# A graph network's node passes become one dense chain, and its edge targets travel as one row per edge

## The chip, the core and the metric

The kernel runs on one core of a Trainium2 chip. The metric is the device time of one execution in microseconds. TensorE (PE) multiplies matrices, VectorE (DVE) and ScalarE (ACT) work elementwise, GpSimd (POOL) issues the indirect DMAs here, and SyncE (SP) issues the plain ones.

## The reference

50,000 nodes with 128 features, 25,000 edges sorted by destination `dst`. Four layers follow one another, each as `x = x + layer(relu(layernorm(x)))`:

```python
h = relu(layernorm(x)); x = x + L0(h)      # GINE
msg = relu(h[src] + edge_attr); agg = segment_sum(msg, dst)
y = relu((h + agg) @ W1.T + b1) @ W2.T + b2;  L0 = batchnorm over nodes(y)

h = relu(layernorm(x)); x = x + L1(h)      # two GATv2 convolutions, 4 heads
for layer in (1, 2):                       # with self loops; h is updated by each
    xl, xr = h @ Wl, h @ Wr                # 128 -> 4 x 128
    e = sum(leaky_relu(xl[src] + xr[dst]) * att); alpha = segment_softmax(e, dst)
    out = segment_sum(alpha * xl[src], dst).mean(heads) + bias
    h = h + layernorm(out) * g + be        # the kernel adds this and applies relu after layer 1

h = relu(layernorm(x)); x = x + L2(h)      # GAT, 4 heads of 64, then an MLP 256 -> 256 -> 128
h = relu(layernorm(x)); x = x + 0.5 * segment_mean(h[src], dst)
```

About 25,000 destinations were drawn from 50,000 nodes, so most nodes have no incoming edge. For such a node every segment sum is zero: its own softmax weight in a convolution is 1, and the attention layer gives it a constant vector.

## The kernel before

Everything is float32. Nodes are padded to 50,176 and handled in 98 tiles of 512 rows (128 partitions x 4), edges to 25,088 in 49 tiles of 512. The program is a sequence of phases, with a barrier after each (`Phase`), so that two phases don't overlap: `prepare_indices`, `gine_edges`, `gine_mlp`, `gine_finish`; for each convolution `conv_logits`, `edge_softmax`, `conv_aggregate`, `conv_nodes`; then `gat_logits`, `edge_softmax`, `gat_aggregate`, `gat_nodes`, and `mean_edges`. Within a phase each engine runs its own stream in order, and semaphores tie them together; `pipeline` writes the steps of several tiles interleaved, each with a lag.

The logits phases gather the rows of both ends of each edge from the table H in DRAM (`gather`, L186, four indirect DMAs of 128 rows for each end), turn them with TensorE transposes, multiply (`z_self`, `z_edge`), and reduce with the attention vectors (`dots`, L862, 32 weight columns for each head, side by side). The aggregate phases weigh the projected rows, turn them, sum each segment with a running scan on DVE (L1213, L1720), turn the sums back and scatter the last row of each segment to the table AGG (`scatter_last`, L192). The node phases (`conv_nodes`, `gat_nodes`) then stream all 98 node tiles: load H and AGG (and X), project and add, normalize, store H (and X). So each layer passes over all nodes once. `mean_edges` adds its rows to `out` with an accumulating indirect DMA (L1880). The attention's MLP runs over the edge tiles inside `gat_aggregate` (L1641, L1651).

A float32 matmul shows in the trace as two instructions, a transpose as one.

## Time and profile before

| | us |
|---|---|
| median of two runs | 6023.07 (6015.77 to 6030.36) |
| span of the profiled execution | 6037.5 |
| PE busy | 3381.0 (56%) |
| DVE busy | 3709.0 (61%) |
| ACT busy | 2564.7 (42%) |
| GpSimd busy | 3636.7 (60%) |

The phases begin at (us from the start of the span): `gine_edges` 28, `gine_mlp` 612, `gine_finish` 943, `conv_logits` 1242.5, `edge_softmax` 1765, `conv_aggregate` 1816, `conv_nodes` 2156; layer 1 of the convolution: 2617, 3138, 3190, 3526; `gat_logits` 4069, `edge_softmax` 4577, `gat_aggregate` 4624, `gat_nodes` 5098, `mean_edges` 5409 to 6037.5. No engine is busy for more than 61% of the whole; the limit is another one in each phase, so the shares of the whole say little and the stages have to be read one by one.

### The profile page before, as it was taken

To read this page: it belongs to the slowest core of one execution; us is meant where nothing else is said; L and a number is where in the kernel's file an instruction comes from. 1 tells how busy PE (TensorE), PEld (TensorE's weight loads), DVE (VectorE), ACT (ScalarE), POOL (GpSimd) and SP (SyncE) were. 2 spreads that over 40 slices of the span, in tenths; PEclk is the share of its full clock that TensorE was granted. 3 is DMA by queue.
4 is the path that set the end of the run, shared out by engine and by line. 5 is a ranking of instruction groups with operands and counts; after the bars stand their busy time and mean duration, and the time that the engine had idled before them with its cause. 6 is when DMAs were issued, how large, how long until landed. Compare 5 with 4: busy or idle time off the path is not lost. (4 is left out here: it accounts for less than half of the span.)

```text
span 6037.5 us, 71358 instructions
## 1 busy us (share of the span) xinstructions
PE 3381.0 (56%) x13980; PEld 1953.5 (32%) x13980; DVE 3709.0 (61%) x10702; ACT 2564.7 (42%) x5746; POOL 3636.7 (60%) x3368
## 2 busy tenths in 40 slices
PE   1221674369968944469978944434445996003332
PEld 0111232223325534423334534421113774002221
DVE  2332898956668979966658969981114555982221
ACT  1222897856641246656651247771111222650100
POOL 4777343467745666667744666657772444448887
PEclk9999996589989977779988966656667998555555
DMA  7332777932214245522212257752221112983343
GB/s 244 93 93 74 234 254 284 368 99 55 55 40 158 80 148 172 173 70 55 55 45 67 79 185 245 248 197 54 54 54 46 53 54 93 341 299 63 61 64 50
DMA packets 531584, 778.51 MB, mean 129 GB/s; under 512 B 162156, under 2 KB 217736, under 8 KB 528752
## 3 DMA queue, kind: packets, MB, share of 16 engines
q1 hardware_dynamic: 427952, 620.88, 30.7%
q0 software_dynamic: 103488, 156.17, 10.8%
q14 instruction: 111, 0.91, 0.0%
q8 instruction: 33, 0.54, 0.0%
HBM read 475.60 MB, written 312.09 MB: 130 GB/s over the span
## 5 line engine op out<-in xcount | busy, mean ns | idle before, releaser
L919 DVE TENSOR_TENSOR conv_logits_leaky<-conv_logits_z,conv_logits_sloped 128x512 f32<-128x512 f32 x784 | 542.4, 692 | 242.9 <-ACT conv_logits_sloped L882 237.6
L1314 PE MATMUL conv_nodes_o_ps<-wmean,conv_nodes_hT 128*128 128x128 f32 x1568 | 318.9, 366 | 454.4 <-ACT conv_nodes_hT L1378 427.0
L882 ACT ACTIVATE conv_logits_sloped<-conv_logits_z 128x512 f32<-128x512 f32 x784 | 468.3, 597 | 220.9 <-PE conv_logits_z L845 119.9
L192 POOL DMA_INDIRECT AGG<-conv_aggregate_rows,conv_aggregate_idx x392 | 385.1, 982 | 261.7 <-ACT conv_aggregate_rows L1177 166.3
L186 POOL DMA_INDIRECT conv_logits_hd<-H,conv_logits_idx x392 | 372.2, 949 | 127.7 <-issue 117.9
L186 POOL DMA_INDIRECT conv_logits_hs<-H,conv_logits_idx x392 | 372.1, 949 | 119.5 <-issue 119.2
L1314 PEld LDWEIGHTS conv_nodes_o_ps<-wmean,conv_nodes_hT 128*128 128x128 f32 x1568 | 271.0, 261 | 519.9 <-ACT conv_nodes_hT L1378 458.9
L1908 PE MATMUL mean_edges_turned<-mean_edges_ident,mean_edges_hs 128*128 128x128 f32 x196 | 54.6, 434 | 685.6 <-DMA mean_edges_hs<-H,mean_edges_idx 685.6
L1286 POOL TENSOR_TENSOR conv_nodes_agg<-conv_nodes_agg,conv_nodes_bias 128x512 f32<-128x512 f32 x196 | 248.5, 1268 | 310.8 <-DVE conv_nodes_scaled L1347 146.2
L1141 PE MATMUL conv_aggregate_y<-wl,conv_aggregate_diff 128*128 128x512 f32 x784 | 393.5, 627 | 31.8 <-DVE conv_aggregate_part L1204 31.8
L246 ACT ACTIVATE conv_nodes_scaled<-conv_nodes_o,conv_nodes_norm_shift,conv_nodes_norm_rstd 128x128 f32<-128x128 f32 x784 | 322.8, 482 | 170.5 <-DVE conv_nodes_norm_shift L241 165.1
L1204 DVE SCALAR_TENSOR_TENSOR conv_aggregate_part<-conv_aggregate_y,conv_aggregate_alpha,conv_aggregate_part 128x128 f32<-128x128 f32 x1176 | 358.5, 347 | 20.6
L845 PE MATMUL conv_logits_z<-conv_logits_hdT,wsum 128*128 128x512 f32 x784 | 366.0, 610 | 1.4 <-ACT conv_logits_hdT L876 1.4
L192 POOL DMA_INDIRECT AGG<-gat_aggregate_rows,gat_aggregate_idx x196 | 192.5, 982 | 268.4 <-ACT gat_aggregate_rows L1673 221.8
L853 PE MATMUL conv_logits_z<-diffT,wl 128*128 (+1 forms) x784 | 352.9, 593 | 0.0
L1880 POOL DMA_INDIRECT out<-mean_edges_rows,mean_edges_idx x196 | 308.1, 1572 | 59.7 <-issue 57.9
L1942 DVE TENSOR_TENSOR_SCAN mean_edges_sumT<-mean_edges_keep,mean_edges_sumT,mean_edges_turned 128x512 f32<-128x512 f32 x49 | 62.7, 1280 | 435.7 <-PE mean_edges_turned L1908 435.7
L1964 ACT ACTIVATE mean_edges_rows<-mean_edges_back,mean_edges_half 128x128 f32<-128x128 f32 x196 | 55.9, 368 | 527.0 <-PE mean_edges_back L1920 286.6
L192 POOL DMA_INDIRECT AGG<-gine_edges_rows,gine_edges_idx x196 | 207.0, 1056 | 102.3 <-issue 100.1
L1908 PEld LDWEIGHTS mean_edges_turned<-mean_edges_ident,mean_edges_hs 128*128 128x128 f32 x196 | 35.0, 217 | 705.1 <-issue 487.7
L1167 ACT ACTIVATE conv_aggregate_alpha<-conv_aggregate_alpha_ps 128x16 f32<-128x16 f32 x98 | 17.9, 183 | 520.8 <-DVE conv_aggregate_part L1204 456.1
L186 POOL DMA_INDIRECT gine_edges_hs<-x,gine_edges_idx x196 | 202.3, 1032 | 61.2 <-issue 58.8
(241 smaller groups left out, 10015.2 us busy)
## 6 DMA issues: line engine op xcount, KB each, us to landing
conv_nodes_h<-H SPq DMA_DIRECT2D x196, 256.0 KB, 2.7
conv_nodes_agg<-AGG SPq DMA_DIRECT2D x196, 256.0 KB, 3.0
AGG<-gine_edges_zero SPq DMA_DIRECT2D x14, 1792.0 KB
gine_mlp_x<-x SPq DMA_DIRECT2D x98, 256.0 KB, 2.7
gine_mlp_agg<-AGG SPq DMA_DIRECT2D x98, 256.0 KB, 3.2
YT<-gine_mlp_yT SPq DMA_DIRECT2D x98, 256.0 KB, 3.2
gine_finish_x<-x SPq DMA_DIRECT2D x98, 256.0 KB, 3.9
gine_finish_yT<-YT SPq DMA_DIRECT2D x98, 256.0 KB, 5.0
```

The source lines that it names most:

```text
L186: return pool.indirect_dma_start(out=out, out_offset=None, in_=table, in_offset=bass.IndirectOffsetOnAxis(ap=index, axis=0))
L192: return pool.indirect_dma_start(out=table, out_offset=bass.IndirectOffsetOnAxis(ap=index, axis=0), in_=rows, in_offset=None, bounds_check ...
L246: last = act.activation(out[:, a, :], x[:, a, :], func, bias=self.shift[k][:, a:a + 1], scale=self.rstd[k][:, a:a + 1])
L845: pe.matmul(z[h][:, :], g.wsum[:, h * D:(h + 1) * D], hdT[slot(k)][:, :], start=True, stop=True).then_inc(z_done[0], 1)
L853: pe.matmul(z[h][:, :], g.wl[:, h * D:(h + 1) * D], g.diffT[:, bass.ds(n * TILE, TILE)], start=False, stop=True, skip_group_check=True).th ...
L882: act.activation(sloped[H * j + h][:, :], z[h][:, :], ACT.Copy, scale=SLOPE).then_inc(sloped_made[j], 1)
L919: dve.tensor_tensor(leaky[H * j + h][:, :], z[h][:, :], sloped[H * j + h][:, :], ALU.max).then_inc(leaky_made[j], 1)
L1141: pe.matmul(y[s][:, :], diff[slot(k)][:, s * P:(s + 1) * P], g.wl[:, :], start=True, stop=True).then_inc(y_done, 1)
L1204: last = dve.scalar_tensor_tensor(out=out, in0=yh, scalar=a, in1=out, op0=ALU.mult, op1=ALU.add)
L1286: pool.tensor_tensor(flat(agg[r]), flat(agg[r]), bias[:, :], ALU.add).then_inc(agg_made, 1)
L1314: last = pe.matmul(o_ps[k % 2][:, a, :], hT[k % 2][:, a * P:(a + 1) * P], g.wmean[:, :], start=True, stop=True)
L1880: pool.indirect_dma_start(out=g.out[:, :], out_offset=bass.IndirectOffsetOnAxis(ap=idx[k][:, 12 + s:13 + s], axis=0), in_=rows[k][:, s, :] ...
```

## The change

Nodes are split in two kinds. A new phase `spread` takes every node through the two convolutions, the attention and the last norm as if it had no incoming edge, in one pass over the 98 node tiles with no return to DRAM between the layers. Nodes with incoming edges are wrong in it and are overwritten: their state is carried as one row per edge (each edge holds a copy of its destination's state), in transposed tiles in DRAM (HDT, X1DT, X2DT), and two new phases, `conv_update` after each `conv_aggregate` and `gat_update` after `gat_aggregate`, update these rows over the 49 edge tiles. `conv_nodes` and `gat_nodes` are gone. `spread` also gathers and turns the destination rows once, and stores for each edge tile the matrix `same` (edge i and j have the same destination) for each block of 128 edges. The aggregates multiply by `same` instead of scanning and scattering; what crosses a block's edge is added in the update phases by small matmuls (`ends`, `ind`). Norms are taken with a centering matrix and a matmul by a column of 1/128, instead of DVE's statistics. A table POS, filled in `gine_finish` by 196 indirect DMAs of 64-byte rows, tells where the current row of a node is; `spread` looks it up for each edge's source (196 more). The logits phases then gather only sources. `conv_logits` splits leaky_relu into a linear part (`lin`, one more matmul) and a relu. `mean_edges` adds the base row on DVE and overwrites rows of `out` with a plain scatter. The loops of the new phases are written out in full, with no loop on the chip. `make_weights` prepares all weights once. `gine_edges` and `gine_mlp` are as before.

```diff
 def gine_finish(nc, g):
...
-                def add_beta(k, i):
-                    pool.tensor_tensor(x1_beta[r][:, :, :], x1[r][:, :, :], beta[:, :, :], ALU.add).then_inc(shifted_made, 1)
+                    if k == 0 and isinstance(i, int) and i == 0:
+                        sp.wait_ge(self_made, 1)
+                        sp.dma_start(g.POS.rearrange("(p j) w -> p j w", p=P), self_row[:, :, :]).then_inc(self_out, 16)
...
+                make_identity(pool, ident, ident_made, cleared)
+                pool.iota(self_row[:, :, :], pattern=[[1, rows_each], [0, 16]], base=0, channel_multiplier=rows_each).then_inc(self_made, 1)
+                pool.iota(edge_row[:, :, :, :], pattern=[[TILE, g.NTE], [1, SUB], [0, 16]], base=g.NP, channel_multiplier=SUB).then_inc(edge_made, 1)
+                pool.wait_ge(self_out, 16)
+                wait_alone(pool, edge_made, 1, own)
+                for n in range(g.NTE):
+                    for s in range(SUB):
+                        scatter_last(pool, g.POS[:, :], g.idx[:, n, 8 + s:9 + s], edge_row[:, n, s, :], g.NP - 1).then_inc(g.placed, 16)
...
+def spread(nc, g):
+                for u in range(E2):
+                    n, col = u // 2, 4
+                    if u >= 7:
+                        wait_alone(pool, e_done, u - 6, own)
+                    for s in range(SUB):
+                        gather(pool, fetched[u % 7][:, s, :], (g.X if u % 2 else g.H)[:, :], g.idx[:, n, col + s:col + s + 1]).then_inc(fetched_in[u % 7], 16)
+                    for s in (0, 1) if u % 2 == 0 else (2, 3):
+                        gather(pool, pos[:, n, s, :], g.POS[:, :], g.idx[:, n, s:s + 1]).then_inc(g.looked, 16)
+                wait_alone(pool, g.looked, 16 * SUB * g.NTE, own)
+                pool.tensor_copy(g.idx[:, :, 12:16], pos[:, :, :, 0]).then_inc(pos_copied, 1)
+                pool.wait_ge(pos_copied, 1)
...
+                def variances(t):
+                    if t == 2:
+                        pe.wait_ge(V_set, 1)
+                    past(pe, sqrt_made, t - 2)
+                    for lag, sq, made, c in ((2, sq0, sq0_made, 0), (5, sq1, sq1_made, 4), (7, sq3, sq3_made, 8), (7, sq2, sq2_made, 12)):
+                        j = t - lag
+                        if 0 <= j < N:
+                            pe.wait_ge(made, j + 1)
+                            for a in range(SUB):
+                                last = pe.matmul(V[:, c + a:c + a + 1], sq[j % 2][:, a * P:(a + 1) * P], g.mean_col[:, :], start=True, stop=True)
+                    last.then_inc(V_done, 1)
...
+                def centered(out, rows):
+                    for a in range(SUB):
+                        last = pe.matmul(out[:, a * P:(a + 1) * P], rows[:, a * P:(a + 1) * P], g.center[:, :], start=True, stop=True)
+                    return last
+                def g3(j):
+                    t = j + 7
+                    past(pe, t0_made, upto(t - 1))
+                    pe.wait_ge(x3_made, j + 1)
+                    alone(t, h4_made, j)
+                    centered(Ga, x3T[j % 3]).then_inc(g3_done, 1)
...
+                def oX(j):
+                    t = j + 6
+                    pe.wait_ge(x3_made, j + 1)
+                    past(pe, sq0_made, upto(t))
+                    alone(t, sq2_made, j)
+                    pe.matmul(Oa[:, :], g.center[:, :], x3T[j % 3][:, :], start=True, stop=True).then_inc(oX_done, 1)
+                def e_turn(u):
+                    if u >= E2:
+                        return
+                    pe.wait_ge(fetched_in[u % 7], fetched0 + 64 * (u // 7 + 1))
+                    past(pe, a0_made, u - 2)
+                    alone(u, a1_made, u - 5)
+                    alone(u, eT_made, u)
+                    turn(T0, flat(fetched[u % 7])).then_inc(e_done, 1)
+                steps = [(6, t1T), (6, x1T), (0, h1T_), (2, g0), (5, g1), (1, out0), (3, t0T), (4, out1), (4, rA_), (7, g3), (7, g2),
+                         (7, r3), (6, oX), (0, e_turn)]
...
+                def squares(j):
+                    act.wait_ge(oX_done, j + 1)
+                    act.activation(sq3[j % 2][:, :], Oa[:, :], ACT.Square).then_inc(sq3_made, 1)
+                    act.activation(sq2[j % 2][:, :], Oa[:, :], ACT.Square, bias=g.ncc[:, :]).then_inc(sq2_made, 1)
+                def copy_e(u):
+                    if u >= E2:
+                        return
+                    act.wait_ge(e_done, u + 1)
+                    past(act, eT_out[u % 3], 16 * (u // 3))
+                    act.activation(eT[u % 3][:, :], T0[:, :], ACT.Copy).then_inc(eT_made, 1)
+                steps = [(0, copy_h1T), (1, square0), (3, relu_a0), (4, square1), (4, copy_rA), (6, squares), (0, copy_e)]
...
 def conv_logits(nc, g, layer):
...
-                        gather(pool, hd[k][:, s, :], g.H[:, :], idx[k][:, 4 + s:5 + s]).then_inc(rows_in[k], 16)
-                        gather(pool, hs[k][:, s, :], g.H[:, :], idx[k][:, s:s + 1]).then_inc(rows_in[k], 16)
+                    for s in range(SUB):
+                        gather(pool, hs[n % 7][:, s, :], table[:, :], g.idx[:, n, col + s:col + s + 1]).then_inc(rows_in[n % 7], 16)
...
+                def dot_edge(n):
+                    past(pe, logit_made[1], n)
+                    pe.matmul(dots[1][:, :], g.lin[layer][:, :, :], g.arena[:, n * TILE:(n + 1) * TILE], start=True, stop=True)
+                    pe.wait_ge(edge_made, n + 1)
+                    pe.wait_ge(edges_made, (H - 1) * (n + 1))
+                    for h in range(H):
+                        last = pe.matmul(dots[1][32 * h:32 * h + 32, :], g.att[layer][:, h, :], above[H + h][:, :],
+                                         start=False, stop=True, tile_position=(0, 32 * h), skip_group_check=True)
+                    last.then_inc(dots_done[1], 1)
+                sweep(N, [(1, z_self), (2, dot_edge), (0, turn), (1, z_edge), (1, dot_self)])
...
 def conv_aggregate(nc, g, layer):
...
+                def project(n):
+                    for s in range(SUB):
+                        past(pe, yw_made, SUB * (n - 1) + s + 1)
+                        pe.matmul(y[s][:, :], g.arena[:, n * TILE + s * P:n * TILE + (s + 1) * P], g.wlc[layer][:, :],
+                                  start=True, stop=True).then_inc(y_done, 1)
+                def collect(n):
+                    pe.wait_ge(same_in[n % 4], 16 * (n // 4 + 1))
+                    past(pe, agg_made, n - 1)
+                    for s in range(SUB):
+                        pe.wait_ge(yw_made, SUB * n + s + 1)
+                        for h in range(H):
+                            last = pe.matmul(agg[n % 2][:, s * P:(s + 1) * P], yw[(SUB * n + s) % 8][:, h * D:(h + 1) * D],
+                                             same[n % 4][:, s * P:(s + 1) * P], start=(h == 0), stop=(h == H - 1))
+                    last.then_inc(agg_done, 1)
+                sweep(N, [(0, turn_alpha), (0, project), (1, collect)])
...
+def conv_update(nc, g, layer):
...
+                def project(n):
+                    pe.wait_ge(hdT_in[n % 6], 16 * (n // 6 + 1))
+                    pe.wait_ge(ind_in[n % 4], 16 * (n // 4 + 1))
+                    past(pe, o_made, n)
+                    pe.matmul(O[:, :], g.wmc[layer][:, :], hdT[n % 6][:, :], start=True, stop=False)
+                    pe.wait_ge(endsT_made, n + 1)
+                    pe.matmul(O[:, :], endsT[n % 2][:, :], ind[n % 4][:, :], start=False, stop=True).then_inc(O_done, 1)
...
+                for at in range(N + 2 + tail + 2):
+                    if 0 <= at - 3 < N:
+                        turn_t(at - 3)
+                    if 2 <= at < N + 2 + tail:
+                        variance(at)
+                    if 0 <= at - 2 < N:
+                        turn_o(at - 2)
+                    if at < N:
+                        turn_ends(at)
+                    if 0 <= at - 1 < N:
+                        project(at - 1)
+                    if final:
+                        if 0 <= at - 5 < N:
+                            center_rows(at - 5)
+                        if 0 <= at - 4 < N:
+                            center_x(at - 4)
+                        if 0 <= at - 6 < N:
+                            turn_rows(at - 6)
+                    elif 0 <= at - 4 < N:
+                        turn_h(at - 4)
...
+def gat_update(nc, g):
...
+                def center_x(n):
+                    pe.wait_ge(x3_made, min(n + 2, N))
+                    pe.matmul(O[:, :], g.center[:, :], x3T[n % 3][:, :], start=True, stop=True).then_inc(X_done, 1)
...
+                sweep(N, [(5, variance), (1, carry(0)), (5, center_rows), (5, turn_x), (1, carry(1)), (2, first), (3, second), (4, center_x), (0, turn_ends)])
...
 def mean_edges(nc, g):
...
-                            pool.indirect_dma_start(out=g.out[:, :], out_offset=bass.IndirectOffsetOnAxis(ap=idx[k][:, 12 + s:13 + s], axis=0),
-                                                    in_=rows[k][:, s, :], in_offset=None, compute_op=ALU.add).then_inc(added[k], 16)
+                        scatter_last(pool, g.out[:, :], g.idx[:, n, 8 + s:9 + s], rows[n % 7][:, s, :], g.NP - 1).then_inc(placed[n % 7], 16)
...
+        steps = [prepare, make_weights, gine_edges, gine_mlp, gine_finish, spread,
+                 lambda nc, g: convolution(nc, g, 0), lambda nc, g: convolution(nc, g, 1), attention, mean_edges]
```

Two places in the program, all on TensorE. First the end of a convolution. Before, the seam between the last edge tile of `conv_aggregate` and `conv_nodes` (`partT` and `back` turn the segment sums there and back, `turned` is a PSUM bank with the turned node tile, `o_ps` the projection):

```order
L1156 MATMUL conv_aggregate_back<-conv_aggregate_ident,conv_aggregate_sumT 128x128 x4
L1148 MATMUL conv_aggregate_partT<-conv_aggregate_ident,conv_aggregate_part 128x128 x4
L1156 MATMUL conv_aggregate_back<-conv_aggregate_ident,conv_aggregate_sumT 128x128 x8
L1082 UNCONDITIONAL_BRANCH
L1297 UNCONDITIONAL_BRANCH
L1306 MATMUL conv_nodes_turned<-conv_nodes_ident,conv_nodes_h 128x128 x8
L1314 MATMUL conv_nodes_o_ps<-wmean,conv_nodes_hT 128x128 x4
L1306 MATMUL conv_nodes_turned<-conv_nodes_ident,conv_nodes_h 128x128 x4
```

Now, at the place of `conv_nodes`, `conv_update` over the 49 edge tiles, here for layer 0 and one tile (R, T and Q are turned rows, F the turned ends, O the projection with what is carried over, V the variance):

```order
L1637 MATMUL conv_update_R<-kept_ident,conv_update_o 128x128 x4
L1644 MATMUL conv_update_F<-kept_ident,conv_update_ends 8x128
L1650 MATMUL conv_update_O<-conv_update_hdT,kept_wmc 128x512
L1652 MATMUL conv_update_O<-conv_update_ind,conv_update_endsT 128x512
L1637 MATMUL conv_update_Q<-kept_ident,conv_update_hT 128x128 x4
L1637 MATMUL conv_update_T<-kept_ident,conv_update_t 128x128 x4
L1663 MATMUL conv_update_V<-kept_mean_col,conv_update_sq 128x1 x4
```

and the node tiles in `spread` (V, Ga, Gb, Oa and Ob are PSUM banks; T stands for T0, T1 and T2 by turns), one tile's turn from the variances on; three groups of four transposes into T stand ahead of it:

```order
L994 MATMUL spread_V<-kept_mean_col,spread_sq 128x1 x16
L956 MATMUL spread_Ga<-kept_ident,spread_o 128x128 x4
L956 MATMUL spread_Gb<-kept_ident,spread_o 128x128 x4
L1014 MATMUL spread_Oa<-spread_h1T,kept_wmc 128x512
L956 MATMUL spread_T<-kept_ident,spread_t 128x128 x4
L1027 MATMUL spread_Ob<-spread_hAT,kept_wmc 128x512
L956 MATMUL spread_T<-kept_ident,spread_hAT 128x128 x4
L1037 MATMUL spread_Ga<-kept_center,spread_x3T 128x128 x4
L1037 MATMUL spread_Gb<-kept_center,spread_x2T 128x128 x4
L956 MATMUL spread_T<-kept_ident,spread_x3T 128x128 x4
L1064 MATMUL spread_Oa<-spread_x3T,kept_center 128x512
L956 MATMUL spread_T<-kept_ident,spread_fetched 128x128 x4
```

Where a node tile had two groups for each convolution, one turn of `spread` now has fifteen, among them sixteen matmuls with one moving column; and the edge tiles got seven groups of their own.

Second, TensorE's stream in the attention. Before, `gat_aggregate`, one tile:

```order
L1614 MATMUL gat_aggregate_alpha_ps<-gat_aggregate_ident,gat_aggregate_alphaT 128x4 x4
L254 REGISTER_ALU
L1623 MATMUL gat_aggregate_y<-wn,gat_aggregate_src 128x256 x4
L1628 REGISTER_ALU
L1632 MATMUL gat_aggregate_partT<-gat_aggregate_ident,gat_aggregate_part 128x128 x8
L254 REGISTER_ALU
L1641 MATMUL gat_aggregate_hid<-gat_aggregate_headsT,gat_aggregate_w 128x512 x4
L1648 REGISTER_ALU
L1651 MATMUL gat_aggregate_o<-gat_aggregate_w,gat_aggregate_hidT 128x128 x8
```

Now the end of it is a phase of its own, `gat_update` (B is the part carried over from neighbouring blocks, G and O the two dense layers, F the turned ends, V the variance, Q and R the outputs):

```order
L2122 MATMUL gat_update_R<-kept_ident,gat_update_x3T 128x128 x4
L2084 MATMUL gat_update_B<-gat_update_ind,gat_update_endsT 128x512
L2092 MATMUL gat_update_G<-gat_update_heads,kept_w 128x512 x4
L2099 MATMUL gat_update_O<-gat_update_hid,kept_w 128x512 x2
L2104 MATMUL gat_update_O<-gat_update_x3T,kept_center 128x512
L2076 MATMUL gat_update_F<-kept_ident,gat_update_ends 8x128 x2
L2110 MATMUL gat_update_V<-kept_mean_col,gat_update_sq 128x1 x4
L2084 MATMUL gat_update_B<-gat_update_ind,gat_update_endsT 128x512
L2116 MATMUL gat_update_Q<-kept_center,gat_update_x3T 128x128 x4
```

The two dense layers (four and two matmuls of 512 columns) moved there, and the carries, the centering, the norm and the last transposes came with them.

## Rows read from the trace of the kernel before

**Rows 1.** Stages: columns as in its head row, (x) instructions; TensorE's granted clock, DMA share, rate.

```profile
core 0: us, PE busy (x) PEld busy (x) DVE busy (x) ACT busy (x) POOL busy (x), PEclk, DMA share, GB/s
612.00:943.00 331.00, 241.29 (x784) 106.66 (x784) 304.76 (x1183) 283.75 (x687) 124.22 (x100) 0.99 0.71 234
943.00:1242.50 299.50, 109.23 (x392) 70.21 (x392) 273.21 (x1080) 249.73 (x588) 124.65 (x101) 0.50 0.96 344
1242.50:1765.00 522.50, 496.95 (x1960) 198.40 (x1960) 306.46 (x447) 322.08 (x540) 374.75 (x395) 0.98 0.20 53
1816.00:2156.00 340.00, 289.11 (x1176) 164.76 (x1176) 288.69 (x837) 62.85 (x147) 196.28 (x200) 0.93 0.32 108
2156.00:2617.00 461.00, 211.28 (x1176) 179.36 (x1176) 438.73 (x1274) 280.00 (x687) 285.67 (x197) 0.74 0.51 169
3526.00:4069.00 543.00, 250.80 (x1176) 215.05 (x1176) 488.46 (x2157) 415.65 (x1079) 364.86 (x296) 0.62 0.70 238
4069.00:4577.00 508.00, 232.01 (x588) 91.50 (x588) 68.58 (x101) 58.01 (x99) 370.50 (x395) 0.66 0.20 53
4624.00:5098.00 474.00, 444.78 (x2352) 330.58 (x2352) 262.50 (x299) 114.91 (x196) 193.02 (x198) 0.97 0.17 51
5098.00:5409.00 311.00, 1.22 (x4) 0.93 (x4) 292.00 (x1184) 182.51 (x491) 130.00 (x98) 0.50 0.93 331
5409.00:6037.50 628.50, 193.83 (x784) 157.27 (x784) 124.96 (x151) 55.88 (x196) 497.20 (x394) 0.50 0.40 62
```

**Rows 2.** Timeline of TensorE, `conv_logits`, one period: start, duration, instruction, count.

```profile
1500.19 1.06 PE L862 MATMUL conv_logits_dots<-conv_logits_leaky,conv_logits_att 128*32 128x512 f32 x8
1501.19 0.66 PE L835 MATMUL conv_logits_hdT_ps<-conv_logits_ident,conv_logits_hd 128*128 128x128 f32 x4
...
1502.12 3.60 PE L853 MATMUL conv_logits_z<-diffT,wl 128*128 x8
1505.64 1.06 PE L862 MATMUL conv_logits_dots<-conv_logits_leaky,conv_logits_att 128*32 128x512 f32 x8
...
1510.27 1.06 PE L862 MATMUL conv_logits_dots<-conv_logits_leaky,conv_logits_att 128*32 128x512 f32 x8
```

**Rows 3.** Timeline of TensorE, `gat_aggregate`, one period.

```profile
4853.53 1.95 PE L1651 MATMUL gat_aggregate_o<-gat_aggregate_w,gat_aggregate_hidT 128*128 128x128 f32 x16
4855.41 1.05 PE L1614 MATMUL gat_aggregate_alpha_ps<-gat_aggregate_ident,gat_aggregate_alphaT 4*128 4x4 f32 x8
4856.39 2.00 PE L1623 MATMUL gat_aggregate_y<-wn,gat_aggregate_src 128*128 128x256 f32 x8
4858.22 1.04 PE L1632 MATMUL gat_aggregate_partT<-gat_aggregate_ident,gat_aggregate_part 128*128 128x128 f32 x8
4859.09 3.60 PE L1641 MATMUL gat_aggregate_hid<-gat_aggregate_headsT,gat_aggregate_w 128*128 128x512 f32 x8
```

**Rows 4.** Timeline of TensorE, `mean_edges`, at the lower clock.

```profile
5704.94 1.86 PE L1915 MATMUL mean_edges_counts_ps<-mean_edges_ident,mean_edges_counts 1*128 1x1 f32 x8
```

**Rows 5.** Timeline of GpSimd, `gine_edges`: a scatter, then a gather.

```profile
303.20 0.98 POOL L192 DMA_INDIRECT AGG<-gine_edges_rows,gine_edges_idx  x1 [0.30 <-issue]
304.49 1.00 POOL L186 DMA_INDIRECT gine_edges_hs<-x,gine_edges_idx  x1 [0.30 <-issue]
```

**Rows 6.** Groups by line: form xcount | busy us, mean ns | idle us before.

```profile
L186 POOL DMA_INDIRECT mean_edges_hs<-H,mean_edges_idx x196 | 188.6, 962 | 61.3 <-issue 59.4 <-DMA mean_edges_idx<-IDX 1.8
L1330 DVE TENSOR_TENSOR conv_nodes_o<-conv_nodes_o_ps,conv_nodes_agg 128x512 f32<-128x512 f32 x196 | 132.4, 676 | 58.6 <-PE conv_nodes_o_ps L1314 33.4 <-issue 21.9 <-POOL conv_nodes_agg L1286 3.3
L635 ACT ACTIVATE gine_mlp_hidT<-gine_mlp_hid,gine_mlp_b 128x512 f32<-128x512 f32 x98 | 65.6, 671 | 1.5 <-PE gine_mlp_hid L604 1.5
L889 ACT ACTIVATE conv_logits_logit<-conv_logits_dots 128x512 f32<-128x512 f32 x196 | 117.0, 597 | 90.0 <-PE conv_logits_dots L862 90.0
L1110 POOL MEMSET conv_aggregate_zero<- 128x3584 f32 x1 | 3.1, 3084 | 0.0
```

**Rows 7.** Timeline of GpSimd, `prepare_indices`.

```profile
0.86 0.56 POOL L145 IOTA prepare_indices_eid<- 128x196 int32 x1 [0.40 <-PEq L126]
```

1963 lines of the change are left out of this document (1081 added, 882 removed).

## The prediction

> **What bounds the kernel now.** I read the stages first: one stretch of the windows view for each phase between two barriers. They hardly overlap, so each has a limit of its own, and the span of 6037.5 us is their sum. In [rows 1], top to bottom: `gine_mlp` (331 us), `gine_finish` (299.5), `conv_logits` of layer 0 (522.5), `conv_aggregate` (340), `conv_nodes` of layer 0 (461), `conv_nodes` of layer 1 (543), `gat_logits` (508), `gat_aggregate` (474), `gat_nodes` (311), `mean_edges` (628.5). The reader should see three kinds. PE-bound: `conv_logits` (PE busy 496.95 of 522.5) and `gat_aggregate` (444.78 of 474). DMA-bound: `gine_finish` and `gat_nodes`, DMA share 0.96 and 0.93 at 344 and 331 GB/s. GpSimd-bound, by issue of indirect DMAs: `gat_logits` and `mean_edges`. The node stages that the change removes, `conv_nodes`, use PE only for 211 and 251 us; DVE is their busiest (438.73 and 488.46).
>
> Then I read one period of TensorE in the two PE-bound stages, since the change gives TensorE nearly all of its new work. Starts of successive groups, no gaps between them, give these prices at the full clock:
> - 4 transposes of 128x128: 0.46 us (8 in 0.93) [rows 2]
> - a float32 matmul of 512 columns: 0.88 (4, shown as 8 instructions, in 3.52) [rows 2]; of 256 columns: 0.46 (1.83 for 4) [rows 3]
> - of 128 columns: 0.235 (8, shown as x16, in 1.88) [rows 3]
> - 128 weight columns but only a few moving columns: 0.245 (4, shown as x8, in 0.98) [rows 3]. So this one costs the same as one of 128 columns.
> - the four narrow `dots` of 32 weight columns together: 1.00 [rows 2].
>
> GpSimd issues a gather every 1.275 us (188.6 + 61.3 over 196) [rows 6] and a scatter every 1.29 (start to start) [rows 5]. A 512-element pass costs 0.68 us on DVE and 0.60 to 0.67 on ACT [rows 6].
>
> **The change part by part.**
>
> *Node stages.* Removed: 461 + 543 + 311 = 1315 us [rows 1]. Added: `spread`, 98 node tiles. PE per tile: 9 groups of 4 transposes (4.14), 3 matmuls of 512 columns (2.64), 8 centering matmuls of 128 columns (1.88), and 16 one-column matmuls for the variances. I have no row with 128 weight rows and one moving column; the bounds are 0, if it hides behind its neighbours, and 0.245. Rows 3 has the same 128 weight columns and a few moving ones, so I take 0.245: 3.92. Sum 12.6. Behind it is one exposed handshake: PSUM bank T0 is used last by the transpose of the fetched rows, ACT empties it (`copy_e`) only after its two squares, and the next turn of the loop begins with T0. From the end of `oX`, ACT needs 0.60 + 0.67 + 0.60, plus about 0.1 for the handoffs (an estimate), while PE has only 0.46 of transposes: 1.5 us of stall. Queued behind that waiting transpose is all of PE's next turn. Period 14.1. DVE (nine passes, 6.5) and ACT (ten passes, 6.6) and GpSimd (6 issues, 7.7) lie beneath it. 98 x 14.1 = 1382; seven more turns to fill and drain at about half: 1425 with the start. Net +110.
>
> *`conv_logits`, twice.* It loses 4 transposes a tile (-0.46) and gains one 512-column matmul (+0.88). The period now is 10.08 [rows 2], so 10.5. The destination gathers go, but GpSimd was below PE, so this is worth nothing. 49 x 0.42 = 21 less some 8 of weight loading: +13 each, +26.
>
> *`conv_aggregate`, twice.* The scan, 8 transposes and GpSimd's scatters go; 16 matmuls of 128 columns come. PE: 4 small (0.98), 4 of 512 columns (3.52), 16 of 128 (3.76) = 8.26 a tile; DVE falls to 4 passes (2.7) and no longer sets the pace. 49 x 8.26 + 15 = 420 against 340: +160 for both.
>
> *`conv_update`, new.* Layer 0, PE: 3 x 0.46, 4 x 0.245, 0.235, 2 x 0.88 = 4.36, and about 0.5 where PE waits: between the projection and the variance of the same tile lie a DVE pass (0.68), an ACT pass (0.60) and some 0.15 of handoffs (an estimate), against 0.92 of transposes: 4.9; 49 turns and the ramp: 268. Layer 1: 1.38 + 8 x 0.245 + 0.235 + 1.76 + 4 x 0.235 + 0.88 = 7.15, all handoffs covered: 390. Together +658. Nothing hides these; they stand where no stage stood.
>
> *Attention.* `gat_logits` keeps 4 of 8 gathers: 49 x 4 x 1.275 + 13 = 263 against 508: -245. `gat_aggregate`: 0.98 + 1.83 + 8 x 0.235 = 4.7 a tile, 253. `gat_update`, PE: 4 x 0.245 + 9 x 0.88 + 4 x 0.235 + 0.46 + 2 x 0.235 = 10.8 (carry 2, first 4, second 2, center 1). Here two handshakes are open: `center_x` needs the bank O that `add_x2` must read first (a DVE pass and a handoff, 0.8), and the variance comes 0.25 too early. 11.85 x 49 + 30 = 611. So 864 against 474: +390.
>
> *`mean_edges`.* The accumulating scatter becomes a plain one: 49 x (5.10 + 5.16) + 14 = 517 against 628.5: -112.
>
> *`gine_finish`.* Its DVE-GpSimd addition goes, worth nothing in a DMA-bound stage. It gains the table POS: SP waits for an iota of 6272 elements between the first and second tile. An iota of 196 took 0.56 [rows 7], which scaled up is 18 us; a fill runs at 3.08 us for 3584 [rows 6], so at least 5.4; I take 12. The store of 3.2 MB at 344 GB/s takes 9. Then 196 scatters of 64-byte rows share the DMA engines. At most they cost as much as 512-byte rows, 64 KB at 53/0.20 = 265 GB/s [rows 1], 0.25 us each, 49 us; at least 0; I take 25, the middle. On GpSimd 196 x 1.29 = 253 still ends inside the stage. +46. The Trainium skill (DMA: Bandwidth & Descriptors, Specifications) says that transfers below 512 bytes do a read-modify-write. By that the upper end, 49, would be the better value and the sum 24 us more; no row here shows such a scatter.
>
> *Preparation.* More loads and passes (+6) and `make_weights`, 21 loads and a chain of small DVE steps, about 28: +34. `gine_edges` and `gine_mlp` are not touched.
>
> Sum: 110 + 26 + 160 + 658 - 245 + (253 + 611 - 474 = 390) - 112 + 46 + 34 = +1067. Against its own execution: 7104. The median of the runs (6023) lies 14 us under that span, so **7090 us**, 18% slower. The change trades memory traffic and GpSimd issues, which had room in the node stages, for float32 TensorE work: about 98 x 12.6 + 49 x (4.4 + 7.2 + 10.8) = 2330 us, of which only the attention's two dense layers (49 x 5.3) were there before.
>
> **The rivals.**
> - *More handshakes are open than I count* (slower still). A turn of `spread` has 15 groups on PE, almost each with a wait of its own, and single PSUM banks. For: `conv_nodes` loses much time between groups. Against: the waits in rows 2 and 3 cost nothing. Price: 8% on the PE-paced new stages (1425 + 840 + 268 + 390 + 253 + 611 + 1070 = 4857): +390, 7480.
> - *The clock falls to 1.2 GHz* in `spread` and the updates, which have small gaps. Eight small instructions took 1.86 there against 1.05 [rows 3, 4], x1.8: 2690 us of stages become about 4800, total near 9200; in the updates alone near 8100. Against: `gine_mlp`, with PE busy for only 241 of 331 us, was granted 0.99, `conv_aggregate` 0.93, while `conv_nodes` at 0.46 busy had 0.74 [rows 1]; the new stages are near 0.9 busy. The Trainium skill (TensorE: Matmul & The Clock Gate, What's actually happening) calls the throttled state the default, which activity lifts; by it both outcomes are possible.
> - *Some stalls are covered* (slower, but less): the T0 stall vanishes (-150) and preparation and POS cost little (-80): 6860.
> - *Faster than before:* independent narrow groups of PE overlap. The four `dots`, each on a quarter of the columns, take 1.00 against 3.52 for full width [rows 2]. If transposes, one-column and 128-column matmuls overlapped 3.5 times too, `spread` would save 7.1 of 14.1 a tile, 695 us, the aggregates 430 and the updates 350: 5610. It decides from a factor of about 2.1. Against: the same shapes run strictly one behind the other in rows 3.
> - *The time doesn't move:* no single cause gives it; the savings of 245 and 112 would have to meet a `spread` of 700 us.
>
> **How the numbers follow.** Forecast 0.62 (own range 6880 to 7350), open handshakes 0.16, lower clock 0.05, covered stalls 0.12, overlap 0.04, something else 0.01. The range 6800 to 7500 holds the first, most of the second and the fourth. About 2% is what a measurement of this kernel can tell from no change: faster 0.03, same 0.02, slower 0.95.
>
> **What would show it.** Right: `spread` near 1425 us with PE over 85% busy at full clock, a wait on ACT's `copy_e` once in each turn, `V` matmuls near 3.9 us for 16, `conv_aggregate` at 420, `gat_update` near 610, `gat_logits` near 260. Wrong: `spread` under 1200 (small matmuls overlap), or over 1550 with waits spread over many lines, or a granted clock under 0.9 there.

## The result, and the profile of the changed kernel

| | before | after |
|---|---|---|
| median of the runs | 6023.07 us | 7438.58 us (7434.15 to 7443.01, 2 runs) |
| ratio to before | 1 | 1.235, 95% interval 1.230 to 1.239 |
| span of the profiled execution | 6037.5 us | 7432.4 us |
| mean granted clock of TensorE | 0.788 | 0.852 |
| TensorE busy | | 5742.2 us, 77% of the span |

The change makes the kernel 23% slower; the forecast was 7090 us, 18% slower, with 7500 as the upper end. The sign was right and so was the main mechanism, float32 work on TensorE setting the pace. The size was a quarter too small: +1395 us between the two spans against the +1067 of the sum. First the head of the page of the kernel after: busy time by engine, then TensorE's busy share and its granted clock in 40 slices, then the row of the one-column matmuls of `spread`.

```profile
span 7432.4 us, 83595 instructions
PE 5742.2 (77%) x27122; PEld 3618.3 (49%) x27122; DVE 2954.1 (40%) x6743; ACT 2105.1 (28%) x4235; POOL 2287.5 (31%) x2285
PE   1214743899999999997999899799996598999333
PEclk9999955888888889998975699899998798889555
L994 PE MATMUL spread_V<-kept_mean_col,spread_sq 128*128 128x1 f32 x3136 | 405.8, 263 | 0.8 <-ACT spread_sq L1120 0.8
```

TensorE is busy nearly everywhere, as forecast. But the clock row holds eights where the busy row holds nines (slices 9 to 15, `spread`), and a five (slice 22, `conv_update` of layer 0) next to a nine. Part of what counts as busy there is the same work at a lower clock.

The windows view by stage answers to [rows 1]. Columns: stretch, length, busy time of PE, PEld, DVE, ACT and POOL with counts, granted clock, DMA share, GB/s. In order: `gine_finish`, `spread`, `conv_logits` 0, `conv_aggregate` 0, `conv_update` 0, `conv_update` 1, `gat_logits`, `gat_aggregate`, `gat_update`, `mean_edges`.

```profile
971.20:1269.10 297.90, 109.10 (x392) 70.09 (x392) 193.84 (x1079) 254.00 (x588) 202.16 (x200) 0.50 0.99 361
1269.10:2822.50 1553.40, 1398.88 (x8820) 1166.01 (x8820) 651.15 (x1035) 605.74 (x1083) 561.89 (x589) 0.85 0.44 151
2822.50:3352.10 529.60, 517.51 (x1862) 195.41 (x1862) 198.87 (x294) 146.33 (x246) 187.12 (x197) 0.99 0.18 51
3403.10:3811.20 408.10, 404.54 (x2352) 302.13 (x2352) 135.56 (x196) 33.15 (x98) 0.00 (x0) 0.99 0.12 33
3811.20:4233.30 422.10, 399.67 (x1274) 223.51 (x1274) 129.86 (x258) 99.25 (x197) 0.00 (x0) 0.57 0.28 94
...
5221.20:5613.10 391.90, 377.79 (x2156) 250.08 (x2156) 201.08 (x359) 99.43 (x200) 0.00 (x0) 0.96 0.49 167
5613.10:5872.50 259.40, 160.27 (x392) 39.27 (x392) 62.74 (x98) 28.77 (x49) 187.11 (x196) 0.81 0.37 101
5919.30:6161.30 242.00, 234.62 (x1568) 216.42 (x1568) 82.30 (x299) 57.91 (x147) 0.00 (x0) 0.97 0.49 162
6161.30:6880.70 719.40, 651.39 (x2058) 313.19 (x2058) 197.48 (x359) 162.62 (x246) 0.00 (x0) 0.88 0.27 91
6880.70:7432.40 551.70, 193.93 (x784) 157.30 (x784) 179.36 (x346) 0.00 (x0) 422.88 (x392) 0.50 0.28 89
```

Against the terms of the sum:

| stage | forecast | measured | difference |
|---|---|---|---|
| `spread` | 1425 | 1553 | +128 |
| `conv_update` 0 | 268 | 422 | +154 |
| `gat_update` | 611 | 719 | +108 |
| `mean_edges` | 517 | 552 | +35 |
| `gine_finish` | 346 | 298 | -48 |
| `conv_aggregate`, both | 840 | 816 | -24 |
| `conv_update` 1 | 390 | 392 | +2 |
| `gat_logits`, `gat_aggregate` | 516 | 501 | -15 |

Three stages hold 390 of the missing time, and they are the three new ones whose granted clock is under 0.9: 0.85, 0.57, 0.88. `conv_update` 1, with the same kinds of instructions, was granted 0.96 and came out to 2 us.

One turn of `spread` on PE, in order of time (start, duration, engine, line, operation, count, idle before it):

```profile
2002.38 0.60 PE L956 MATMUL spread_T<-kept_ident,spread_fetched 128*128 128x128 f32 x4
2004.35 0.63 PE L956 MATMUL spread_T<-kept_ident,spread_t 128*128 128x128 f32 x4 [1.36 <-issue]
2004.81 0.60 PE L956 MATMUL spread_T<-kept_ident,spread_x 128*128 128x128 f32 x4
2005.25 0.60 PE L956 MATMUL spread_T<-kept_ident,spread_h 128*128 128x128 f32 x4
2005.68 3.72 PE L994 MATMUL spread_V<-kept_mean_col,spread_sq 128*128 128x1 f32 x32
2009.27 1.09 PE L956 MATMUL spread_Ga<-kept_ident,spread_o 128*128 128x128 f32 x4
...
2011.01 1.77 PE L1014 MATMUL spread_Oa<-spread_h1T,kept_wmc 128*128 128x512 f32 x2
2012.61 0.60 PE L956 MATMUL spread_T<-kept_ident,spread_t 128*128 128x128 f32 x4
```

And the windows view of the same kernel, cut at 2009.0 and 2012.5:

```profile
2004.00:2009.00 5.00, 4.65 (x43) 4.68 (x43) 1.99 (x3) 0.85 (x2) 3.78 (x5) 1.00 0.96 320
2009.00:2012.50 3.50, 3.50 (x13) 2.58 (x14) 1.64 (x3) 0.27 (x1) 1.73 (x2) 0.51 0.93 290
2012.50:2019.00 6.50, 5.53 (x37) 4.13 (x35) 2.73 (x4) 4.95 (x9) 0.15 (x1) 1.00 0.02 5
```

The forecast wait is there: 1.36 us before the first transpose into T0. The row gives "issue" as its releaser, since it shows no semaphore event; what is late there is `copy_e`, which the first experiment bears out. What was not forecast comes after it. Once the sixteen one-column matmuls are through (2009.2), the granted clock is at half, 1.2 GHz, for three and a half microseconds: four transposes take 1.09 instead of 0.60 and the projection 1.77 instead of 1.02. Then full speed is back. The dip shown is a short one: in the steady part of `spread` (1380 to 2792 us) the clock falls 68 times, 50 of them for 6.8 us, and each time between 2.2 and 3.7 us behind the start of a turn's one-column matmuls. Turns without such a dip take 13.38 us from start to start; with one, 13.9 to 16.4. The mean of all is 15.2.

So at this point two things could be the cause: the wait (theory A), which was my reading of the clock rival ("small gaps"), or the one-column matmuls (theory B).

### The profile page after: what moved, and what is told of

Read it like the earlier page. It is cut to its first block and busy times, and to the rows that moved or that the text cites. A ratio compares the mean times of both kernels' runs of the same rounds, so it can differ in the third digit from the quotient of the medians.

```text
span 7432.4 us, 83595 instructions
## 1 busy us (share of the span) xinstructions
PE 5742.2 (77%) x27122; PEld 3618.3 (49%) x27122; DVE 2954.1 (40%) x6743; ACT 2105.1 (28%) x4235; POOL 2287.5 (31%) x2285
## 5 line engine op out<-in xcount | busy, mean ns | idle before, releaser
L1555 DVE TENSOR_TENSOR conv_aggregate_yw<-conv_aggregate_y,conv_aggregate_alpha 128x512 f32<-128x512 f32 x392 | 271.1, 692 | 535.5 <-PE conv_aggregate_y L1518 528.9
L994 PEld LDWEIGHTS spread_V<-kept_mean_col,spread_sq 128*128 128x128 f32 x3136 | 408.2, 213 | 1.7 <-issue 1.6
L994 PE MATMUL spread_V<-kept_mean_col,spread_sq 128*128 128x1 f32 x3136 | 405.8, 263 | 0.8 <-ACT spread_sq L1120 0.8
L1527 PEld LDWEIGHTS conv_aggregate_agg<-conv_aggregate_same,conv_aggregate_yw 128*128 128x128 f32 x3136 | 365.3, 192 | 45.9 <-issue 45.9
L1314 ACT ACTIVATE conv_logits_above<-conv_logits_z 128x512 f32<-128x512 f32 x392 | 234.0, 597 | 497.5 <-PE conv_logits_z L1278 497.5
L1518 PE MATMUL conv_aggregate_y<-kept_wlc,arena 128*128 128x512 f32 x784 | 367.8, 612 | 0.0
L1278 PE MATMUL conv_logits_z<-conv_logits_hdT,kept_wsum 128*128 128x512 f32 x784 | 366.5, 611 | 0.0
L1527 PE MATMUL conv_aggregate_agg<-conv_aggregate_same,conv_aggregate_yw 128*128 128x128 f32 x3136 | 365.6, 275 | 0.0
L1285 PE MATMUL conv_logits_z<-arena,kept_wl 128*128 128x512 f32 x784 | 352.9, 593 | 0.0
L307 POOL DMA_INDIRECT out<-mean_edges_rows,kept_idx x196 | 231.3, 1180 | 59.7 <-issue 59.1
```

The source lines that it names most:

```text
L307: return pool.indirect_dma_start(out=table, out_offset=bass.IndirectOffsetOnAxis(ap=index, axis=0), in_=rows, in_offset=None, bounds_check ...
L994: last = pe.matmul(V[:, c + a:c + a + 1], sq[j % 2][:, a * P:(a + 1) * P], g.mean_col[:, :], start=True, stop=True)
L1278: pe.matmul(z[h][:, :], g.wsum[layer][:, h * D:(h + 1) * D], hdT[n % 4][:, :], start=True, stop=True).then_inc(z_done[0], 1)
L1285: pe.matmul(z[h][:, :], g.wl[layer][:, h * D:(h + 1) * D], g.arena[:, n * TILE:(n + 1) * TILE], start=False, stop=True, skip_group_check=T ...
L1314: act.activation(above[h][:, :], z[h][:, :], ACT.Relu).then_inc(self_made, 1)
L1518: pe.matmul(y[s][:, :], g.arena[:, n * TILE + s * P:n * TILE + (s + 1) * P], g.wlc[layer][:, :], start=True, stop=True).then_inc(y_done, 1)
```

## Experiments

The code cuts are shortened: names stand for longer expressions, and the semaphore counts that follow a new order are left out. Most kernels below ran once. What a single run of a stage can tell is seen from those that leave the stage alone: `spread` took 1548 to 1553 us in them, `conv_update` 0 422 to 424, `gat_update` 716 to 727, `gine_finish` 292 to 301, `mean_edges` 549 to 552.

### The wait of spread taken away

```
-  (7, r3), (6, oX), (0, e_turn)]                    # PE
+  (7, r3), (0, e_turn), (6, oX)]
-  (4, copy_rA), (6, squares), (0, copy_e)]          # ACT
+  (4, copy_rA), (0, copy_e), (6, squares)]
```

> Edit: in spread, PE transposes the fetched rows (e_turn) before oX instead of after it, and ACT copies them (copy_e) before its two squares. The work is the same; the wait of 1.36 us in each turn before the first transpose goes. In the kernel after, a turn of spread takes 13.38 us where the granted clock stays at full speed, 15.23 on the mean, with 0.85 granted. Theory A, the wait brings the clock down: turn 12.0 us, granted clock above 0.97, stage 1553 -> about 1235, whole kernel about 7120. Theory B, the clock falls whatever is done about the wait (the sixteen one-column matmuls and the narrow groups bring it down): turn about 13.9, granted clock still about 0.85, stage about 1420, whole kernel about 7305.

Measured: 7242.68 us in one run. The stage `spread`:

```profile
1270.10:2630.40 1360.30, 1330.61 (x8820) 1093.35 (x8820) 649.48 (x1035) 616.10 (x1083) 567.82 (x589) 0.87 0.50 172
```

PE is busy for 1330.6 of 1360.3 us: there is almost no wait left, and yet the clock stands at 0.87. As the cause, theory A falls. But the wait had a part in it. Every steady turn still has a dip, now of 3.4 us, where most had lasted 6.8. So the gain, 193 us, is the wait itself, 98 x 1.36 = 133, which is all that B gave, and some 60 us of clock. The step of the forecast that put this wait behind `copy_e` holds: both its place and its length were right.

### Three quarters of the one-column matmuls left out

```
-  for a in range(SUB):
+  for a in range(1):
       last = pe.matmul(V[:, c + a:c + a + 1], sq[j % 2][:, a * P:(a + 1) * P], g.mean_col[:, :], start=True, stop=True)
```

> Edit: in spread only the first of the four one-column matmuls of each variance group is made (4 instead of 16 a turn); twelve columns of V keep the value 1, so this leaves out the variance of three nodes in four of each tile. The 1.36 us wait at the turn's start stays. Priced at full clock by its rows, one such matmul takes 0.22 us. Theory A (the wait sets the clock): granted clock stays under 0.88, mean turn about 12.3, stage 1553 -> about 1265. Theory B (the one-column matmuls set it): clock above 0.95, turn about 10.8, stage about 1120. If such matmuls hid behind their neighbours, less than 0.1 us each would be saved and the stage would stay above 1430.

Measured: 6970.41 us, one run. The stage `spread`:

```profile
1274.30:2358.80 1084.50, 927.60 (x6468) 746.45 (x6468) 635.14 (x1035) 601.18 (x1083) 560.95 (x589) 0.98 0.63 216
```

The wait of 1.36 us is still in every turn and the clock is at 0.98. Every turn of the steady part takes 10.70 us. Theory B holds for `spread`. The price also follows: 13.38 - 10.70 = 2.68 us for twelve matmuls, 0.223 each, where I had taken 0.245. They hide behind nothing, so the overlap rival is excluded. Of the 469 us that this saves, 98 x 2.68 = 263 are the matmuls' own time and the other 206 are clock.

### The sixteen split up

```
+  if t >= 2 and step is x1T:  variances(t, (0,))      # four of them here
+  if t >= 2 and step is h1T_: variances(t, (1,))      # four here
   if step is g0 and t >= 2:   variances(t, (2, 3))    # eight where sixteen stood
```

> Edit: in spread the sixteen variance matmuls no longer stand in one run. Four come after the first transposes of the turn, four after the second, eight where all sixteen stood. Same work, same number. Theory C1 (an unbroken run of 3.5 us is what counts): granted clock above 0.95, turn about 13.4, stage 1553 -> about 1345, whole kernel about 7230. Theory C2 (their share of the turn counts, wherever they stand): clock 0.85, stage about 1550, whole kernel about 7440.

Measured: 7467.08 us, one run; `spread` took this long:

```profile
1271.90:2858.20 1586.30, 1433.57 (x8820) 1200.08 (x8820) 652.34 (x1035) 604.08 (x1083) 560.61 (x589) 0.82 0.44 148
```

Not better but 33 us worse, at 0.82. An unbroken run of sixteen is not what it takes; eight still stand together here.

### More columns in each

Each variance matmul moves 32 equal columns instead of one; number, place and waits stay.

```
-  V[:, c + a:c + a + 1] <- sq[...], g.mean_col [P, 1]
+  V[:, c + a, :]        <- sq[...], g.mean_col [P, 32]      # V is [P, 16, 32]
```

> Edit: every one-column variance matmul (spread, both conv_update, gat_update) multiplies with 32 equal columns of 1/128 instead of one, and the square root reads one column in 32 of the result. Count, order and waits are unchanged. In the run with four instead of sixteen such matmuls the granted clock in spread was 0.98 against 0.85, so these matmuls bring it down. Theory C (it is that almost nothing streams through the array while they run): each still takes 0.22 us, the clock comes back above 0.95 in spread, whose turn is 13.4 us, stage 1553 -> about 1345; update0 422 -> about 280; gat_update 719 -> about 650; whole kernel about 7020. Theory D (any dense run of short matmuls does it, however many columns): clock 0.85, spread 1550, whole kernel about 7440. If 32 columns make each matmul longer by 0.1 us, spread gains 1.6 us a turn on top.

Measured: 7268.42 us, one run. `spread`, `conv_update` 0, `gat_update`:

```profile
1270.30:2660.80 1390.50, 1235.35 (x8820) 1047.55 (x8820) 647.09 (x1035) 602.22 (x1083) 560.70 (x589) 0.95 0.50 169
3648.80:4056.40 407.60, 380.80 (x1274) 210.41 (x1274) 129.91 (x258) 99.26 (x197) 0.00 (x0) 0.62 0.28 97
5983.40:6717.30 733.90, 666.33 (x2058) 323.24 (x2058) 197.57 (x359) 162.58 (x246) 0.00 (x0) 0.86 0.26 89
```

Half an answer. In `spread` most turns are back at 13.38 us, but of every five or six one or two still dip (14.7, now and then 16.4); in the other two stages little moved: `conv_update` 0 gained 15 us, and `gat_update` lost 15, of which 7 lie beyond what it took in any run that leaves it alone. So I took the width of every other matmul of these stages, 128 columns. In `spread` there is no room for 16 x 128 columns in PSUM, so each result is written over the surplus of the one before it (24 columns apart) and only its first column is read.

```
-  V[:, c + a:c + a + 1] <- sq[...], g.mean_col [P, 1]
+  V[:, 24 * (c + a):24 * (c + a) + P] <- sq[...], g.mean_col [P, P]
```

> Only the 128 moving columns of the variance matmuls, in the order of the kernel after. With 32 columns spread took 1390 us at 0.95 granted, update0 408 at 0.62, gat_update 734 at 0.86. Theory C: spread's clock above 0.98 with the 1.36 us wait still in each turn, turn 13.6, stage about 1370; the wait alone then costs its own length and no clock. In update0, where the block ends' short matmuls (8 rows or 8 weight columns) stay as they are: between 300 (they don't matter) and 400 (they keep the clock at 0.6). gat_update about 670 or 730 in the same way. Whole kernel about 7240.

Measured: 7035.02 us, one run. The same three stages:

```profile
1264.40:2610.30 1345.90, 1188.97 (x8820) 1011.30 (x8820) 645.13 (x1035) 601.95 (x1083) 563.15 (x589) 0.99 0.52 174
3598.30:3893.00 294.70, 256.67 (x1274) 146.92 (x1274) 130.02 (x258) 99.30 (x197) 0.00 (x0) 0.95 0.40 134
5823.80:6482.60 658.80, 590.79 (x2058) 282.12 (x2058) 197.51 (x359) 162.59 (x246) 0.00 (x0) 0.97 0.30 99
```

More work for TensorE, 404 us less time. Nothing was reordered, no wait was removed, and the three clocks went from 0.85, 0.57 and 0.88 to 0.99, 0.95 and 0.97. Each steady turn of `spread` takes 13.43 us, wait included. In `conv_update` 0 the steady turns take 5.52 us, all alike; what is left under full clock are the first 30 us and the last few. The short matmuls of the block ends (8 rows or 8 weight columns), which stayed, were not the cause in `conv_update` 0. This is the experiment that shows the price of the clock: 1553 - 1346 = 207 us, 422 - 295 = 127 us, 719 - 659 = 61 us, together 395. What it is in a wider matmul that keeps the clock up, no run here tells apart; the width alone was changed.

The Trainium skill (TensorE: Matmul & The Clock Gate, HAM oscillation — how this bites in real kernels) explains a clock that goes up and down by waits of TensorE for data. That alone doesn't describe these runs: without the wait `spread` stayed at 0.87, and with the wait and wider matmuls it was at 0.99.

### The waits of the update stages

`conv_update` 0 doesn't have short dips like `spread`. Its clock stays at half for about 30 us at a time, with TensorE busy all the while, and is at full speed for 3.4 us in between. One such stretch of the kernel after:

```profile
3982.10:4012.70 30.60, 30.60 (x90) 17.05 (x89) 8.82 (x18) 6.49 (x14) 0.00 (x0) 0.50 0.27 98
```

In a turn at full clock the variance waits for a pass on DVE and a square on ACT, 0.48 us in the rows of the kernel after:

```profile
4014.20 0.60 PE L1637 MATMUL conv_update_T<-kept_ident,conv_update_t 128*128 128x128 f32 x4
4015.28 1.13 PE L1663 MATMUL conv_update_V<-kept_mean_col,conv_update_sq 128*128 128x1 f32 x8 [0.48 <-ACT conv_update_sq L1727]
```

```
   turn_t(at - 3)
-  variance(at)
   turn_o(at - 2)                # now waits for o itself
   turn_ends(at)
+  variance(at)
```

> Edit: in conv_update of layer 0 the four variance matmuls come after the transposes of o and of the block ends, so that the pass on DVE and the square on ACT have time to finish. Same work. In the kernel after, the stage takes 421 us at a granted clock of 0.57, and the variance waits 0.48 us in a turn. Theory A (a wait in each turn brings the clock down): the wait goes, granted clock above 0.95, turn about 4.4 us, stage about 260, whole kernel about 7280. Theory B (the mix of short matmuls brings it down, wait or not): granted clock stays at 0.55 to 0.60, stage about 400, whole kernel about 7415.

Measured: 7338.39 us, one run; the stage:

```profile
3813.10:4132.10 319.00, 305.30 (x1274) 179.43 (x1274) 129.87 (x258) 99.19 (x197) 0.00 (x0) 0.76 0.36 124
```

Between the theories: 319 us, where A gave 260 and B 400. With less waiting the clock was at its upper level for more of the stage (0.57 to 0.76), but not for all of it: turns of 4.82 us stand beside turns of up to 9.0. The reordering also changes which matmuls stand beside the variance, which this run doesn't tell from the wait. So here the order counts as well as the columns.

In `gat_update` the centering matmul waits for DVE to read the bank it writes (0.84 us a turn), and the variance comes 0.15 us early:

```
-  (1, carry(1)), (2, first), (3, second), (4, center_x), (0, turn_ends)      # PE
+  (1, carry(1)), (4, center_x), (2, first), (3, second), (0, turn_ends)
-  (5, root), (1, relu_heads), (2, hidden), (4, square)            # ACT
+  (5, root), (1, relu_heads), (4, square), (2, hidden)
```

> Edit: in gat_update the centering matmul of x3 moves ahead of the first dense layer, so that it no longer waits for add_x2 of the tile just projected, and ACT squares before its two relus. Same work. In the kernel after, the stage takes 720 us at 0.88 granted, a turn 12.68 us at full clock and 14.13 on the mean, with waits of 0.84 and 0.15 us in it. Theory A: waits go and the clock comes back to above 0.97, turn 11.7, stage about 600, whole kernel about 7320. Theory B: only the waits go, clock about 0.88, stage about 671, whole kernel about 7390.

Measured: 7381.7 us, one run; the stage:

```profile
6160.80:6830.20 669.40, 650.15 (x2058) 320.53 (x2058) 193.28 (x359) 159.85 (x246) 0.00 (x0) 0.84 0.29 98
```

669 us against 671 from B: the waits go, and the clock, if anything, gets worse (0.88 to 0.84).

One-column matmuls alone are not enough either. `conv_update` 1, in the kernel after, has eight of them in a turn, and they take 1.7 of its 7.42 us. Yet in its steady part TensorE was granted full speed throughout, with hardly a wait:

```profile
5260.00:5605.00 345.00, 344.50 (x2056) 233.48 (x2056) 185.85 (x325) 92.88 (x188) 0.00 (x0) 1.00 0.51 173
5309.26 0.95 PE L1663 MATMUL conv_update_V<-kept_mean_col,conv_update_sq 128*128 128x1 f32 x8
5310.07 1.03 PE L1663 MATMUL conv_update_V<-kept_mean_col,conv_update_sqX 128*128 128x1 f32 x8
```

The first line is the windows view, the other two the timeline of one turn. Why this stage is spared, while `gat_update` with four of them in a turn of 12.7 us is not, stays open.

### Two smaller terms

```
-  for n, s: scatter_last(pool, POS, ...)                      # gine_finish: left out
-  rows = back * half + base     # mean_edges, on DVE
+  rows = back * half            # on ACT; base is loaded and not added
```

> Two edits in stages that don't meet. (1) mean_edges: the rows are made by ACT from PSUM with the scale alone (the term carried in BASE is loaded but not added), instead of by DVE with the addition. In the kernel after, three of four scatters of a tile take 0.98 us and the fourth 1.9, and the stage 552 us. Theory M (the fourth shares the time of DVE's passes that write the rows): it falls to 1.0, turn 11.24 -> about 10.3, stage about 507. Rival: the scans of DVE, which stay, are what it meets: stage stays at 545 to 552. (2) gine_finish: the 196 scatters into POS are left out (the table keeps each node's own row, so later gathers read the source node's row and not the edge's). I had priced them at 25 us of the stage; the stage as a whole took 298. Theory P (they ride in gaps of the queues): stage 290 to 300. Rival: stage about 270.

Measured: 7411.92 us, one run. First line `gine_finish`, second `mean_edges`:

```profile
970.60:1257.90 287.30, 109.13 (x392) 70.11 (x392) 193.82 (x1079) 254.44 (x588) 10.58 (x4) 0.50 0.98 369
6863.10:7410.10 547.00, 193.86 (x784) 157.29 (x784) 124.08 (x150) 56.02 (x196) 418.36 (x392) 0.50 0.28 89
```

The 196 scatters into POS cost 298 - 287 = 11 us against the kernel after, and 5 to 14 us against all the runs that keep them (292 to 301): about what theory P says, and under my 25. In `mean_edges` the fourth scatter still takes up to 1.88 us, and the stage 547 us, so theory M falls: it isn't the pass that writes the rows. That leaves the scans. In the kernel after, two of the four scatters of a tile and the two scans:

```profile
7010.32 1.28 DVE L2282 TENSOR_TENSOR_SCAN mean_edges_sumT<-mean_edges_keep,mean_edges_sumT,mean_edges_turned 128x512 f32<-128x512 f32 x1 [7.27 <-issue]
7010.36 0.98 POOL L307 DMA_INDIRECT out<-mean_edges_rows,kept_idx  x1 [0.30 <-issue]
7011.52 1.25 DVE L2285 TENSOR_TENSOR_SCAN mean_edges_counts<-mean_edges_keep,mean_edges_counts,mean_edges_two 1x512 f32<-1x512 f32 x1
7011.65 1.91 POOL L307 DMA_INDIRECT out<-mean_edges_rows,kept_idx  x1 [0.30 <-issue]
```

A scatter that starts behind the first scan takes 0.98; one that starts behind the second takes 1.91. The first scan reads one input from PSUM, the second both from SBUF. The Trainium skill (SBUF — State Buffer, Who interferes with whom) says that a DVE instruction with two SBUF inputs contends with a GpSimd instruction that reads SBUF. By that rule the cure is to lay the constant row `two` into PSUM. It went into the last kernel.

### All of it together

The three reorderings with 32 columns first:

> The three reorderings of e1, e2 and e3 together with the 32 columns of e7; the result is the reference's. Theory C: spread 98 turns of 12.0 us, about 1200 us; update0 about 255; gat_update about 600; whole kernel about 6810, still 13% over the kernel before. Theory D (columns don't matter): the reorderings alone, spread 1360, update0 319, gat_update 669: about 7095.

Measured: 6908.46 us (4 runs), ratio to before 1.143, interval 1.139 to 1.147. `spread` and `conv_update` 0:

```profile
1269.00:2582.80 1313.80, 1285.04 (x8820) 1077.13 (x8820) 650.61 (x1035) 613.31 (x1083) 567.73 (x589) 0.90 0.53 178
3571.40:3837.10 265.70, 251.94 (x1274) 146.89 (x1274) 129.92 (x258) 99.11 (x197) 0.00 (x0) 0.93 0.43 149
```

`conv_update` 0 came out at 266, near the 255 of theory C; `spread` did not (1314 against 1200): six or so turns of 11.89 us alternate with a dozen or so at 13.5. Against the run with 32 columns and the old order, the order alone took `conv_update` 0 from 408 to 266 us (0.62 to 0.93) and `gat_update` from 734 to 590 (0.86 to 0.97), far more than the waits themselves, 24 and 49 us. With 32 columns the order decides over the clock in these two stages; with 128, as the next run shows, it hardly does.

Then with 128 columns and the row in PSUM:

```
-  two = m.sb("two", [1, TILE])
+  two = m.ps("two", [1, TILE])
```

> The three reorderings again, the variance matmuls now with 128 moving columns each (the results overlap in PSUM, each later one writes over the surplus of the one before, the first column of each stays), and in mean_edges the constant row that the counting scan adds lies in PSUM instead of SBUF. The result is the reference's. Theory C (columns that stream decide the clock): with 32 columns spread was granted 0.90 and took 1314 us; with 128 the clock is above 0.97, a turn 12.1 us and the stage about 1215. Theory D' (it is the short matmuls as such, a larger width changes nothing more): 0.90 and about 1315. Theory M2 for mean_edges (a DVE instruction with both inputs in SBUF holds up GpSimd's scatter): with one input in PSUM the fourth scatter falls from 1.9 to 1.0 us, stage 550 -> about 507. Rival: stage stays at 550. Whole kernel about 6750 where both hold, 6905 where neither does.

Measured: 6753.54 us (4 runs), ratio to before 1.118, interval 1.113 to 1.124. `spread`, `conv_update` 0, `gat_update`, `mean_edges`, and a scatter behind the second scan:

```profile
1265.70:2475.10 1209.40, 1178.43 (x8820) 1005.97 (x8820) 644.82 (x1035) 611.76 (x1083) 568.64 (x589) 0.99 0.58 194
3463.90:3719.80 255.90, 241.34 (x1274) 141.68 (x1274) 129.91 (x258) 99.19 (x197) 0.00 (x0) 0.96 0.46 155
5648.50:6242.20 593.70, 574.40 (x2058) 286.25 (x2058) 193.22 (x359) 157.57 (x246) 0.00 (x0) 0.97 0.34 110
6242.20:6755.50 513.30, 193.63 (x784) 157.46 (x784) 178.95 (x346) 0.00 (x0) 384.52 (x392) 0.50 0.33 95
```
```profile
6611.54 1.24 DVE L2288 TENSOR_TENSOR_SCAN mean_edges_counts<-mean_edges_keep,mean_edges_counts,mean_edges_two 1x512 f32<-1x512 f32 x1
6611.72 0.98 POOL L307 DMA_INDIRECT out<-mean_edges_rows,kept_idx  x1 [0.30 <-issue]
```

Both theories hold: every steady turn of `spread` takes 11.94 us, and the fourth scatter fell from 1.91 to 0.98, the stage from 552 to 513. It had been 550 in the run before this one, with the same order; no scatter takes more than 1.02 us now. The trace agrees with that rule. This kernel is 685 us faster than the changed one, computes the same, and is still 12% slower than the kernel before. That rest is what the change costs by its own plan: with clock and waits mended, `spread` 1209, the two `conv_update` 256 and 391 and `gat_update` 594 make 2450 us of node and update work, where 1315 us of node stages and the dense layers inside `gat_aggregate` stood. None of the versions beats the kernel before.

## Why the prediction was right, and where not

- **Direction and main mechanism: right.** Memory traffic and GpSimd issues are traded for float32 matmuls on TensorE, and TensorE sets the pace of every new stage. The changed kernel's PE was busy for 90% of `spread`, 95% of `conv_update` 0, 91% of `gat_update`.
- **The prices of the matmuls: right, a little high.** A one-column matmul costs 0.223, not 0.245 (and not 0); four transposes 0.44, not 0.46. That a turn of `spread` with the wait and an undisturbed clock takes 13.38 us (14.1 forecast) is the sum of these and of the wait, 0.14 shorter than forecast.
- **The wait on T0: right.** 1.36 us against 1.5, once a turn, at the place named.
- **The clock: this is the step that failed.** I gave "the clock falls to 1.2 GHz" 5%, and imagined it as all or nothing: 9200 us, or 8100. I argued against it with busy share alone, "the new stages are near 0.9 busy". What happened is between: dips of a few microseconds behind the one-column matmuls in `spread` (0.85) and `gat_update` (0.88), and stretches of 30 us at half clock in `conv_update` 0 (0.57). The forecast's own sign of being wrong, a granted clock under 0.9 in `spread`, came true. The "small gaps" that I named in that rival had a part (some 60 us of clock in `spread`), but with 128 columns and the gaps in place the stages were granted 0.95 to 0.99. Price 207 + 61 + 127 = 395 us, in three terms that I had put at full clock. With the clock restored those three terms measured 1346 + 295 + 659 = 2300 us; forecast was 1425 + 268 + 611 = 2304. The sum was 328 us short; this step is worth 395, and the other terms together came out 67 us under the forecast. The warning stood in [rows 1]: stages at 0.62, 0.66 and 0.74, which is neither level but a mixture of both. A partial clock was ordinary in this kernel, and I reasoned only with its two ends.
- **Open handshakes: not the cause.** It gave +390 too, nearly the right size, for the wrong reason. The measured 7438 us lie above the forecast's own range (6880 to 7350) and inside the stated one only because that was drawn wide enough for this rival; that is luck. No wait was found that the forecast didn't name; the two in `gat_update` and `conv_update` 0 were named, at 0.8, 0.25 and 0.5 us, and measured 0.84, 0.15 and 0.48. Removing all waits at the restored clock saves 137 + 39 + 65 = 241 us.
- **`gat_update` was short by 48 us even at full clock** (659 against 611): the three matmuls of 512 columns that stand alone between other groups took 1.05 us each where I had 0.88 from long rows of equal ones [rows 2], 0.5 of the 0.8 us that a turn is over; the rest is spread over the other groups. `spread` was long by 79, and the two hide each other in the sum above.
- **`conv_logits`, `conv_aggregate`, `conv_update` 1, `gat_logits`, `gat_aggregate`: right** to 5%.
- **`mean_edges`: mechanism right, size off.** The plain scatter is cheaper than the accumulating one (0.98 against 1.57 us), but every fourth meets the counting scan. About 11.2 us a tile instead of 10.26. The group of the accumulating scatters in the kernel before (mean 1572 ns):

```profile
L1880 POOL DMA_INDIRECT out<-mean_edges_rows,mean_edges_idx x196 | 308.1, 1572 | 59.7 <-issue 57.9 <-DMA mean_edges_idx<-IDX 1.8
```

- **`gine_finish`: +46 forecast, -1.6 measured.** The iota took 6.65 us, not 12, and the scatters cost about 11 (5 to 14), not 25. The Trainium skill (DMA: Bandwidth & Descriptors, Specifications) made the upper end of 49 the better value; the measurement is against it. Without the scatters the stage is 12 us shorter than before the change in spite of the table's store. What of it is the addition that went, I priced at nothing and did not test.

## What to carry to other kernels

A busy TensorE is not a fast TensorE: read the granted clock beside the busy share for each stage, and where it lies between 0.5 and 1, cut the turn at the dip and look at which matmuls stand just ahead of it. Then change those matmuls and the waits apart from each other and together. Here they were matmuls with one moving column, and giving each the 128 columns of its neighbours, work whose result nobody reads, took 404 us off the kernel. And where GpSimd issues DMAs back to back, try one input of the DVE instructions beside it in PSUM; here that was worth 38 us.

## What the runs showed of the hardware that was not expected

- With the same instructions in the same order, the moving columns of the variance matmuls alone took the granted clock of `spread` from 0.85 (1 column) over 0.95 (32) to 0.99 (128), that of `conv_update` 0 from 0.57 over 0.62 to 0.95. At full clock a matmul with 128x128 weights cost about 0.22 us with 1, 32 or 128 columns.
- Neither waits nor one-column matmuls alone settle the clock. `conv_update` 1, with eight of them in each turn and hardly a wait, was granted full speed for 345 us; `conv_update` 0, with four in a turn, was at half clock for 30 us on end while TensorE was busy without a break.
- Dips need no wait: 98% busy, 0.87 granted. And a reordering that only removes waits can lower the mean clock (`gat_update`, 0.88 to 0.84).
- With 32 columns the turns fell into a pattern: without the wait, four to six of 11.89 us and then a dozen or so of 13.5; with the wait, one or two slow turns in five or six. Why it repeats in that way stays open.
- A DVE scan with both inputs in SBUF lengthened a GpSimd scatter from 0.98 to 1.91 us; with one of them in PSUM it did not.
